# The last stage of a two-layer Fourier kernel: a loop over seven images on four engines, written out as straight code for eight

## What is computed

```python
# layer 0
x = x + conv0(gn(x))   # rfftn, 16x16 modes mixed by complex weights, irfftn; plus x @ skip_kernel + skip_bias
# layer 1
x = x + conv1(gn(x))   # rfft2, 32x32 modes times fw1 and fw2, irfft2 -> out; relu(out @ W + b + out)
return x
```

## Time and profile before

| | |
|---|---|
| median of 3 runs | 2326.72 us |
| the runs | 2326.9, 2320.53, 2326.72 us |
| profiled execution, its own time | 2320.88 us |
| its span, first to last instruction | 2319.0 us |
| mean granted TensorE clock | 0.871 |
| TensorE busy, matmul / weight load | 1832.5 us (79%) / 1464.1 us (63%) |
| VectorE, ScalarE, GpSimd busy | 1463.5 us (63%), 1120.3 us (48%), 263.9 us (11%) |
| DMA queue of the transfers | 515.47 MB, 67.9% of 16 engines' time |
| last stage | from about 1210 us to the end |

### The profile page before, as it was taken

One profiled execution on the slowest core, in us unless ns is written; L12 is line 12 of the kernel. 1 busy time (PEld: TensorE's weight loads), 2 busy tenths in 40 slices (PEclk: granted clock), 3 DMA queues, 4 the chain that ended last, 5 costly groups with the idle time before them and its releaser, 6 DMA issues. The chain is left out here.

```text
span 2319.0 us, 60510 instructions
## 1 busy us (share of the span) xinstructions
PE 1832.5 (79%) x24234; PEld 1464.1 (63%) x24234; DVE 1463.5 (63%) x2219; ACT 1120.3 (48%) x1852; POOL 263.9 (11%) x476
## 2 busy tenths in 40 slices
PE   5898999997296433343547999999999999999999
PEld 3676767776155333233445777877777787777887
DVE  5876767772447211114555777877777887777887
ACT  5665556661143000001335666666665676656665
POOL 0000000001003000000451301203030120303000
PEclk9999999998555655556778999999999999999999
DMA  8887887872956999996644878878788787878886
GB/s 298 308 265 239 260 258 260 274 240 45 191 74 148 276 270 257 255 257 178 228 148 160 313 278 289 301 258 311 278 317 291 265 296 268 315 278 312 304 289 261
DMA packets 240503, 586.24 MB, mean 253 GB/s; under 512 B 71171, under 2 KB 160771, under 8 KB 203907
## 3 DMA queue, kind: packets, MB, share of 16 engines
q1 hardware_dynamic: 163778, 515.47, 67.9%
q10 hardware_dynamic: 71040, 60.70, 10.3%
q0 software_dynamic: 5376, 5.76, 0.9%
HBM read 381.01 MB, written 168.30 MB: 237 GB/s over the span
## 5 line engine op out<-in xcount | busy, mean ns | idle before, releaser
L1299 ACT ACTIVATE x_turned<-ps_xt 128x512 f16<-128x512 f32 x512 | 305.6, 597 | 370.8 <-PE ps_xt L1387 370.8
L1342 DVE TENSOR_TENSOR x_turned<-ps_xt,x_turned 128x512 f16<-128x512 f32 x512 | 351.7, 687 | 137.9 <-ACT x_turned L1299 137.9
L1431 PE MATMUL ps_y<-apply,x_turned 128*128 (+1 forms) x6144 | 431.1, 221 | 0.0
L1431 PEld LDWEIGHTS ps_y<-apply,x_turned 128*128 128x128 f16 x6144 | 380.6, 99 | 64.8 <-issue 1.1
L221 DVE TENSOR_TENSOR parts<-stage,parts 128x1024 f16<-128x1024 f32 x256 | 302.1, 1221 | 108.4 <-ACT parts L145 107.9
L1363 DVE SCALAR_TENSOR_TENSOR y_out<-ps_y,relu 128x512 f32<-128x512 f32 x512 | 351.6, 687 | 20.1 <-PE ps_y L1431 3.2
L1387 PE MATMUL ps_xt<-c_eye,x_in 128*128 128x128 f32 x2048 | 314.7, 277 | 45.3 <-issue 28.8
L1309 ACT ACTIVATE relu<-ps_wave 128x512 f32<-128x512 f32 x512 | 303.4, 593 | 14.5 <-PE ps_wave L1417 14.2
L145 ACT ACTIVATE parts<-stage 128x1024 f16<-128x1024 f32 x256 | 255.1, 1049 | 76.9 <-issue 40.8
L1334 DVE SCALAR_TENSOR_TENSOR low_tile<-ps_col,high_tile 128x512 f16<-128x512 f32 x256 | 176.8, 692 | 120.4 <-ACT high_tile L1293 120.4
L290 PE MATMUL row_ps<-parts,c_rows_dft 128*64 128x512 f16 x1536 | 201.4, 390 | 63.1 <-DVE parts L221 54.1
(11 more groups left out here) (121 smaller groups left out, 1973.2 us busy)
## 6 DMA issues: line engine op xcount, KB each, us to landing
stage<-in_x SPq DMA_DIRECT2D x256, 512.0 KB, 4.9
x_in<-in_x SPq DMA_DIRECT2D x128, 1024.0 KB, 8.5
out_y<-y_out SPq DMA_DIRECT2D x128, 1024.0 KB, 5.0
fw_first<-in_fw SPq DMA_DIRECT2D x9, 2048.0 KB, 19.7
fw<-in_fw ACTq DMA_DIRECT2D x8, 2048.0 KB, 24.0
fw<-in_fw SPq DMA_DIRECT2D x8, 2048.0 KB, 20.3
fw_first<-in_fw ACTq DMA_DIRECT2D x7, 2048.0 KB, 20.8
raw<-mixed ACTq DMA_DIRECT2D x12, 1024.0 KB, 7.2
```

What stands on the lines that cost most here:

```text
L1299: nc.scalar.activation(turned[u % 2][:, 0, :, :], ps_turn[u % 2][:, :, :], ACT.Copy).then_inc(turn_high, 1)
L1342: nc.vector.tensor_tensor(v[:, 1, :, :], ps_turn[u % 2][:, :, :], v[:, 0, :, :], ALU.subtract).then_inc(turn_split, 1)
L1431: mm = nc.tensor.matmul(ps_y[u % 2][:, :, 2 * k:2 * k + 2], turned[u % 2][:, p, k, :], apply[:, bass.ds(b, 1), q, :, :].rearrange("p o c w ...
```

## The change

On SyncE, ScalarE, VectorE and TensorE the loop over seven images and the call for the eighth become one loop of the generating program over eight. Everything in it is emitted eight times, with `b` a plain number, so every wait compares with a constant and every address is fixed. There is no branch left within the stage. The order of the work within an image is the same. GpSimd's part is not touched.

```diff
@@ SyncE
             fill_tiles(0, 0)
-            with sp.Fori(0, B - 1) as b:
-                image(b, False)
-            image(B - 1, True)
+            for b in range(B):
+                image(b, b == B - 1)
@@ ScalarE
             split(0, 0)
-            with act.Fori(0, B - 1) as b:
-                image(b, False)
-            image(B - 1, True)
+            for b in range(B):
+                image(b, b == B - 1)
@@ VectorE
             split(0, 0)
-            with dve.Fori(0, B - 1) as b:
-                image(b, False)
-            image(B - 1, True)
+            for b in range(B):
+                image(b, b == B - 1)
@@ TensorE
             turn(0, 0)
-            with pe.Fori(0, B - 1) as b:
-                image(b, False)
-            image(B - 1, True)
+            for b in range(B):
+                image(b, b == B - 1)
```

## The result

The changed kernel took 2289.36 us (median of 4 runs, 2288.08 to 2299.85), against 2326.81 us for the kernel before. The ratio is 0.9857 with a 95% interval of 0.9832 to 0.9883, so 27 to 39 us less, 33 in the middle. The profiled execution has a span of 2287.4 us where that of before has 2319.0.

A forecast was written before the change was run, and what follows sets the result against it. The prediction took the last stage to run at TensorE's own rate, with stalls at its loop's jumps back. Gains of 41.3 + 3 = 44 us (41 to 48) gave a forecast of 2281 us, range 2272 to 2291.

The forecast's parts named there:

- Part 1: TensorE's jumps back between images go: 41.3 us gained over six crossings, 28.8 of stalls and 12.5 more.
- The weighing of the branch figure: At TensorE's jumps, 51 and 108 ns per branch would make six worth 0.65 us; the trace's 4.6 to 5.3 was preferred.
- Part 2: Jumps back of ScalarE, VectorE and SyncE go: costed at nothing, as they stand beside TensorE's own.
- Part 3: Register arithmetic before waits goes on TensorE, ScalarE and VectorE: covered by matmuls, units stay 2.21 us, so nothing.
- Part 4: SyncE's register arithmetic before the x load behind tile copies and planes goes: about 3 us gained, bounds nothing to 7.
- Part 5: Instruction supply in the last stage, code of seven images read once each: nothing on the path.
- The partial rival: Without idle time at crossings, transfers lag and mid-image waits for x grow: 12 to 30 us come back, 2294 to 2312; chance 9%.
- main term: The gain from removing TensorE's jumps back at the six crossings between images: 41.3 us.

The follow-up runs named there:

- the short jump: Changed kernel plus a two-turn loop around one already met wait on TensorE at each of the seven crossings between images; ratio 0.9868, stage 1042.6 us.
- the pause: Changed kernel plus a 30-turn loop around one already met wait on TensorE at each of the seven crossings between images; ratio 1.0276.

## Why the prediction was right or wrong

- **Part 1, TensorE's back edge: right, in place and size.** The crossings give the 41.3 us to the last tenth, since all seven look like the earlier trace rows. (What the prediction calls the sixth group after the last one is the sixth counted with it.) With the late load out of the way the stage shows 39.8. The clock behaved as said.
- **The weighing of the branch figure: right.** The Trainium skill's 51 and 108 ns ("Advanced Engine Details and Errata", "Control Flow Timing") fit the short jump, which can't be seen; they don't fit the jump to the top of a body of thousands of instructions. That the fetch of far code makes the difference is the reading of its page "Runtime: NRT & Kernel Launch", section "Instruction fetch mechanics", and the traces agree: an instruction packet ends 1.5 to 1.8 us before the end of each of TensorE's 18 stalls. The prediction said that no row shows the fetch; the trace of before has it, at every jump.
- **Part 2, the other engines: right for this change,** since they were changed too. "Nothing" is not their worth by themselves: left in a loop, ScalarE or VectorE takes back 19 to 22 us, because the lead of TensorE over them is some 2 us and a jump is 5.
- **Part 3: right.** The transposes' period is 2.21 us as before.
- **Part 4, SyncE at the late load: wrong, and this is the step that failed.** I took 3 us of gain, with bounds of 0 and 7. The pauses went as said, but the term has the other sign: the waits, with their slow units, took 7.3 us more (28.0 against 20.7). The lower bound of nothing was no bound: I priced only what SyncE does before the issue and took the landing time of the load as given. With TensorE in the loop and SyncE written out the waits are 17.5 us, so the term as I defined it measures about nothing (-1.0); with TensorE written out they are 19.0 to 23.2.
- **Part 5, instruction supply, "nothing on the path": wrong, and the other half of the same step.** I looked at how many packets there are and not at when they move. The packets went from 107 and 74 to 92 and 38, so their number was not the matter. A packet in a load's flight costs that load 1 to 2 us, straight code puts packets into the flight of the load after chunk 3 in images 2, 4 and 7, and the late load stands behind it. That this is the whole of the 7.3 us isn't shown.
- **The rivals.** The partial rival's effect came, with 7.3 us for its lowest price of 12, but its mechanism did not: the pause shows that the transfers need no rest.
- **The range.** 41.3 + 3 = 44 was expected. The crossings' 41.3 less 7.3 leave the 34.0 of the stage, and the ratio says 33 (27 to 39). The range's high end allowed a main term 5 us short for any reason, and not a part 4 with the opposite sign on top.

## What to carry to other kernels

Here a loop with a long body cost about 5 us per jump back on each of three engines, and an engine's stall was hidden as long as another stood at its own jump: write out all coupled engines or none. A trace often holds the sample for such an edit, here the one crossing that fell through, and it gave the main term exactly; the miss came from the place where a transfer was already late, so a wait that stands in the profile before deserves a bound on the worse side too, even where the edit seems to help it. And the late transfer was worth nearly as much as the loops, 28 us of stage time against 34: issuing 1.5 MB of planes two chunks earlier, where little was queued, took away all seven waits.

## What the runs showed of the hardware

- A jump to the top of a long body: 4.4 to 5.3 us on TensorE, ScalarE and VectorE alike. An instruction packet starts 1.8 to 3.6 us into the stall, and 1.4 to 1.8 us after its end the engine goes on. A jump over three instructions: no gap with 2 turns. With 30 turns TensorE stood idle for 9.4 to 9.6 us, some 0.3 us per turn (an estimate, 9.5 / 30).
- After a wait of 7.17 us, as after the stalls, four transposes took 1.11 us in place of 0.61; the granted clock was 0.50 over 1705 to 1707 us, while TensorE was still idle.
- 128 more semaphore increments in a row on TensorE (256 against 128) lengthened its wait at the stage's start from 34.4 to 54.3 us, 0.16 us each.
- One packet of TensorE's instructions in the flight of a 1 MB load made it land in 7.8 to 9.2 us in place of 6.9 (26 loads against 24 of 25). In straight code the place of these packets differs from image to image and moves with 128 instructions of filler; in the loop it is the same in each.
